# A decoder layer's cross-attention: ScalarE writes the key mask into PSUM in eight of twelve score slots

## The chip, the core and the metric

The kernel runs on one core of a Trainium2 chip. The time is the device time of one execution in microseconds (us). The core has five engines that run their own instruction streams and meet at semaphores: TensorE (PE: matmul; PEld: its weight loads), VectorE (DVE), ScalarE (ACT), GpSimd (POOL) and SyncE (SP, which here issues the DMAs). A matmul writes PSUM, which has 8 banks.

## What is computed

32 sequences ("rows" below) of 112 tokens and width 256 pass through a decoder layer: a delta-rule attention with an MLP, a cross-attention over 375 context positions with 16 heads of 16, and a mixture of 6 experts with top-2 routing beside a shared expert. The change is in the cross-attention:

```python
x = x + attn(layernorm(x))
# cross-attention, 16 heads of width 16
Q, K, V = split(h @ wq.T), split(ctx @ wk.T), split(ctx @ wv.T)
scores = Q @ K.T / sqrt(16)
scores = where(mask == 1, -1e9, scores)          # mask: (32, 112, 375)
x = x + (softmax(scores) @ V) @ w_out.T
x = x + shared(h3) + top2_of_6_experts(h3)
```

## The kernel before

The cross-attention stage takes the rows one after another, about 19 us each, from 501 us to 1094 us of the profiled span. The scores are built transposed, keys on partitions: 375 keys are three chunks of 125, 16 heads are four groups of four, so a row has 12 **slots** (`SLOTS`), each a score tile of 125 keys x (4 heads x 112 queries) = 448 columns in one PSUM bank. Even slots use bank 0, odd slots bank 1.

In each slot PE (`mask_scores`, L1127 on, matmul at L1137) first multiplies `negbig` (a diagonal of -2^40, bf16) by `flagk` (the mask of this key chunk as 0 or 1, repeated over 4 heads), which opens the bank's accumulation with the masked value. Two matmuls of 224 columns (`score`, L1142) then add the scores of two head pairs each. ScalarE (`exponentials`, L1644) turns the tile into exponentials in SBUF (`pr`, six buffers). After four slots PE multiplies them by the values (`weighted_values`, L1156; in slots 1, 5 and 9 of the stream, for the four slots that lie one to four before). The mask matmul of slot q has to wait until the exponentials of slot q-2, which read the same bank, are done.

Each engine's order is written out by hand in its `step`. Into the slots of row r PE weaves, in fixed places, work of its neighbours: 16 row-maximum matmuls (L1122) for row r+1, whose tiles VectorE reduces (L2174); the projections of keys (L873 in slots 1 and 2), queries (slot 5, L1091) and values (slot 8, L873) for row r+2; and the end of row r-1: the transpose of its values' sum (slot 3, L1170), the transpose of its normalised output (slot 6, L1177) and the output projection (slot 7, `project_out`, L1184). PE runs its stream strictly in this order, so a wait in front of one of these holds up all that stands behind it.

ScalarE's order in a row, one place after another:

- slot 0: hT copy (L1660), exp 0; slot 1: exp 1, the copy of the values' sum (L1649), high half of the keys 0 (L1619)
- slot 2: exp 2, high half of the keys 1; slot 3: exp 3, the gate's exp (L1664); slot 4: exp 4, h2T copy (L1623)
- slot 5: exp 5, high half of the queries (L1627); slot 6: exp 6, onT copy (`copy_on`, L1653), for which the output projection waits
- slot 7: exp 7; slot 8: exp 8, negated maxima (L1638), values (L1632)
- slot 9: values (L1634), high half of the context (L1542), exp 9; then exp 10 and exp 11

VectorE makes the low half of keys 1 (`klo`, L2160) out of ScalarE's high half; the transpose of h in slot 4 (L1083) waits for that.

The last row (row 31) has no row after it, so there are no row maxima in it, and ScalarE has six more instructions in its slots 3 to 8 (`high_expert`, L1676, a weight piece each, which GpSimd or VectorE then splits). Behind row 31 come the routing of the last rows, the plan of the expert blocks and the experts.

Of the kernel before, what the change touches and what calls it, by code (L numbers as in the profile page):

```python
# [33 lines left out]
ACT = mybir.ActivationFunctionType  # L34
# [7 lines left out]
B, T, D = 32, 112, 256  # L42
# [20 lines left out]
G = B // GB  # L63
GT = GB * T
# [3 lines left out]
KP = S2 // KC  # L68
# [4 lines left out]
LEVELS = (2, 4, 8, 16, 32, 64)  # L73
SLOTS = KC * HEADS // 4
PROBS = 6
BIG = float(2 ** 40)
# [4 lines left out]
RB = 3  # L81
ROUNDS = (B - 3) // RB
DENSE = (3, 7)
HPB = 4
FIRST_MAXIMA = 2
MAXIMA = ((0, 0, 0, 0), (1, 1, 1, 0), (1, 1, 0, 1), (0, 1, 0, 0), (1, 0, 0, 0), (1, 1, 1, 0), (1, 0, 0, 1), (0, 1, 0, 0))
LN_EPS, RMS_EPS = 1e-5, 1e-6

# [35 lines left out]
def decoder_layer(nc, io, out):  # L124
    with ExitStack() as ctx:
# [3 lines left out]
        def sem(name):  # L129
            return ctx.enter_context(nc.semaphore(name))  # L130
# [3 lines left out]
        bank = [psum[:, i, :] for i in range(8)]  # L134
# [89 lines left out]
        with ExitStack() as scope:  # L224
# [18 lines left out]
            flagk = w2("flagk", [KP, RB, KC, T], BF16)  # L243
# [16 lines left out]
        with ExitStack() as scope:  # L260
# [42 lines left out]
        s = {n: sem(n) for n in names + [f"stage{i}" for i in range(STAGES)]}  # L303
        s2 = {n: sem("c_" + n) for n in """cleared ctx_in c_hi c_lo mask_in ready bn flags stat rs h hT_ps hT_sb q_ps q_hi q_lo k_ps k_hi k_lo v01_ps v_ps v_sb qst0 qst1 qst2 kst0 kst1 kst2
            max_ps smax mt_ps negm negm_in sc_ps exp pv_done pv_sb ot_ps rden on onT_ps onT_sb wo_ps x_new""".split()}
# [72 lines left out]
        def heads_at(q, place):  # L378

            n = FIRST_MAXIMA + sum(sum(x) for x in MAXIMA[:q]) + sum(MAXIMA[q][:place])  # L380
            return range(n, n + MAXIMA[q][place])

# [12 lines left out]
        def ahead(t, par, rows):  # L395

            return t + (par + rows) // RB, (par + rows) % RB
# [459 lines left out]
        def _(pe):  # L857
# [250 lines left out]
            def row_max(t, par, heads):  # L1108

                n = t * RB + par  # L1110
                for hd in heads:
                    if hd == 0:
                        pe.wait_ge(s2[f"qst{par}"], filled("qst", t))
                        pe.wait_ge(s2[f"kst{par}"], filled("kst", t))
                        if not is_row(n, 0):
                            pe.wait_ge(s2["negm"], n)
                        if not isinstance(n, int) or n >= 4:
                            pe.wait_ge(s["h1"], G + n - 2)
                    freed = 2 if is_row(n, 0) else 3
                    if hd >= freed:  # L1120
                        pe.wait_ge(s2["smax"], HEADS * n + hd - freed + 1)
                    pe.matmul(bank[max_bank(n, par, hd)][0:T, 0:S2E], head(qst[par][0:ROWS], hd), pair(kst[par][0:ROWS], hd // 2), start=True, stop=True).then_inc(s2["max_ps"], 1)  # L1122
# [6 lines left out]
            def mask_scores(t, par, q):  # L1129

                b = t * RB + par
                if q == 0:
                    pe.wait_ge(s2["negm_in"], 16 * (b + 1))
                    pe.wait_ge(s2["flags"], b + 1)
                pe.wait_ge(s2["exp"], SLOTS * b + q + 2)
                flags = flagk[:, par, q // HPB, :].unsqueeze(1).broadcast_to([KP, HPB, T])
                pe.matmul(bank[q % 2][0:KP, 0:GT], negbig[:], flags, start=True, stop=False, skip_group_check=True)  # L1137
# [78 lines left out]
            def step(t, par, first=False, following=2):  # L1216
# [3 lines left out]
                if following >= 1:  # L1220
                    row_max(*nxt, range(FIRST_MAXIMA))
                if early >= 2:
                    transpose_row(*ahead(t, par, -2))
                for q in range(SLOTS):

                    maxima = following >= 1 and q < len(MAXIMA)
                    mask_scores(t, par, q)
                    for i in range(HPB // 2):
                        score(t, par, q, i)
# [241 lines left out]
        def _(act):  # L1471
# [65 lines left out]
            def high_context(t, par):  # L1537
                f = t * RB + par
                act.wait_ge(s2["ctx_in"], 16 * (f + 1))
                if not is_row(f, 0):  # L1540
                    act.wait_ge(s2["v_ps"], f)
                nc.scalar.copy(chi[:, :, 0:S2], ctxT[:]).then_inc(s2["c_hi"], 1)  # L1542
# [69 lines left out]
            def high_k(t, par, m):  # L1612
                f = t * RB + par
                act.wait_ge(s2["k_ps"], DC * f + m + 1)
                if m == 0 and not is_row(f, 0):
                    before = ahead(t, par, -1)
                    act.wait_ge(s2[f"kst{before[1]}"], filled("kst", before[0]))
                    act.wait_ge(s2[f"qst{before[1]}"], filled("qst", before[0]))
                nc.scalar.copy(khi[:, m], bank[DENSE[m]][:, 0:S2E]).then_inc(s2["k_hi"], 1)  # L1619

            def copy_h(t, par):
                act.wait_ge(s2["hT_ps"], t * RB + par + 1)
                nc.scalar.copy(h2T[:], bank[DENSE[1]][:, 0:2 * T]).then_inc(s2["hT_sb"], 1)  # L1623
# [5 lines left out]
            def copy_v(t, par, part):  # L1629
                act.wait_ge(s2[("v01_ps", "v_ps")[part]], t * RB + par + 1)  # L1630
                if part == 0:
                    nc.scalar.copy(vaug[par][:, 0:2, :, 0:HD], bank[DENSE[1]][0:KP, :].rearrange("k (c h d) -> k c h d", c=2, d=HD)).then_inc(s2["v_sb"], 1)  # L1632
                else:
                    nc.scalar.copy(vaug[par][:, 2, :, 0:HD], bank[DENSE[0]][0:KP, 0:D].rearrange("k (h d) -> k h d", d=HD)).then_inc(s2["v_sb"], 1)  # L1634
# [5 lines left out]
            def exponentials(t, par, q):  # L1640
                done = SLOTS * (t * RB + par) + q
                act.wait_ge(s2["sc_ps"], done + 1)
                act.wait_ge(s2["pv_done"], done + 1)
                nc.scalar.activation(pr[q % PROBS][:].rearrange("k i q -> k (i q)"), bank[q % 2][0:KP, 0:GT], ACT.Exp, scale=1.0 / HD ** 0.5).then_inc(s2["exp"], 1)  # L1644

            def copy_pv(t, par):
                p = t * RB + par
                act.wait_ge(s2["pv_done"], SLOTS * (p + 1) + PROBS)
                nc.scalar.copy(pv[:], bank[6][:, 0:GT]).then_inc(s2["pv_sb"], 1)  # L1649
# [5 lines left out]
            def keep_h(t, par):  # L1655
                r = t * RB + par
                act.wait_ge(s["ht_ps"], G + r + 1)
                if not isinstance(r, int) or r >= 3:
                    act.wait_ge(s3["sent"], 16 * (r - 1))
                nc.scalar.copy(hT3[par][:], bank[DENSE[0]][:, 0:2 * T]).then_inc(s3["hall"], 1)  # L1660
# [17 lines left out]
            def step(t, par, first=False, following=2, context=True):  # L1678
                early = t * RB + par if isinstance(t, int) else RB
                prev, nxt, far = ahead(t, par, -1), ahead(t, par, 1), ahead(t, par, 2)  # L1680
                for q in range(SLOTS):
                    if q == 0 and early >= 2:
                        keep_h(*ahead(t, par, -2))
                    if q == 9 and following >= 2:
                        copy_v(*far, 1)
                    if q == 9 and context:
                        high_context(*ahead(t, par, 3))
                    exponentials(t, par, q)
                    if q == 1 and not first:
                        copy_pv(*prev)  # L1690
                    if q in (1, 2) and following >= 2:
                        high_k(*far, q - 1)
                    if q == 4 and following >= 2:
                        copy_h(*far)
                    if q == 5 and following >= 2:
                        high_q(*far)
                    if q == 6 and not first:
                        copy_on(*prev)
                    if q == 8 and following >= 1:
                        negate_max(*nxt)  # L1700
                    if q == 8 and following >= 2:
                        copy_v(*far, 0)
                    if q == 3 and early >= 2:
                        exponential_gate(*ahead(t, par, -2))
                    if early == 1 and q in (5, 7, 9):
                        high_expert((q - 5) // 2)
                    if following == 0 and 3 <= q < 3 + NE:
                        high_expert(q)
# [136 lines left out]
        def _(dve):  # L1845
# [344 lines left out]
            def step(t, par, first=False, following=2, norm=True):  # L2190
# [4 lines left out]
                if following >= 1:  # L2195
                    maxima(*nxt, range(FIRST_MAXIMA))
                for q in range(SLOTS):
                    for place in range(4):
# [7 lines left out]
                        if place == 0 and q == 3 and following >= 2:  # L2206
                            low_k(*far, 1)
                        if following >= 1 and q < len(MAXIMA):
                            maxima(*nxt, heads_at(q, place))
# [279 lines left out]
```

## Time and profile before

| | before |
|---|---|
| time, median of 3 runs | 1362.65 us (1361.55 to 1363.04) |
| time of the profiled execution | 1365.04 us |
| its span, first to last instruction | 1363.0 us |
| PE busy / PE weight loads busy | 1260.6 us (92%) / 1146.1 us (84%) |
| DVE / ACT / POOL busy | 906.5 (67%) / 652.5 (48%) / 511.7 us (38%) |
| mean granted TensorE clock | 0.974 |

Busy time adds up the durations of an engine's instructions, and for PE overlapping matmuls are joined. An instruction's duration is its own latency, not what it costs the engine: in the timeline the next one often starts before it ends. A start of one to the start of the next is the cost. The chain of waits is the path of work that ended last, and gives each instruction on it only the time by which it held the path.

### The profile page before, as it was taken

The page shows a single profiled execution, that of the slowest core. Times are in us where ns is not written, and L with a number is a line of the kernel's source. Part 1 is how long each engine was busy: PE and PEld are TensorE (multiplying, and loading weights), DVE is VectorE, ACT ScalarE, POOL GpSimd, SP SyncE. Part 2 cuts the span into 40 slices and gives each one's busy share as a digit, 9 for nine tenths or more (in the row PEclk, how much of TensorE's full clock was granted, in tenths as well). Part 3 has the DMA queues.
Part 4 walks back from the last instruction along what each step waited for, and adds up shares of the span by engine and source line. Part 5 has one row for each costly group of instructions (what it writes and reads, how often), then busy time and mean ns, then how long its engine had stood idle before and what let it go on. Part 6 is the DMA issues. An engine that isn't in the chain of part 4 may idle for free.

```text
span 1363.0 us, 34519 instructions
## 1 busy us (share of the span) xinstructions
PE 1260.6 (92%) x11122; PEld 1146.1 (84%) x11122; DVE 906.5 (67%) x2932; ACT 652.5 (48%) x1524; POOL 511.7 (38%) x709
## 2 busy tenths in 40 slices
PE   4899999999989779999999999999999987999994
PEld 4789989889878678998999999999999876888883
DVE  3785674764854557777777777777777576655547
ACT  3443344334333325555555555555555653555540
POOL 2332241331431243244443444444344361333336
PEclk9999999999999889999999999999999998999997
DMA  8499600000000334555555555555555343333358
GB/s 200 107 236 240 149 0 0 0 0 0 0 12 11 87 103 120 147 143 142 129 140 132 144 142 133 131 135 144 142 140 145 76 136 86 99 106 101 102 137 247
DMA packets 131262, 151.39 MB, mean 111 GB/s; under 512 B 41107, under 2 KB 111108, under 8 KB 131156
## 3 DMA queue, kind: packets, MB, share of 16 engines
q1 hardware_dynamic: 124436, 134.55, 40.4%
q0 software_dynamic: 6160, 15.69, 3.4%
q8 instruction: 42, 0.69, 0.2%
q14 instruction: 48, 0.39, 0.1%
q10 hardware_dynamic: 576, 0.07, 0.0%
HBM read 79.27 MB, written 45.82 MB: 92 GB/s over the span
## 4 chain that ended last, share of the span: by engine, by line
PE 51%; DVE 4%; DMA 2%; POOL 2%; issue 2%; SPq 1%; ACT 1%; DVEq 0%; POOLq 0%; ACTq 0%
PE psum L873 9%; PE psum L1122 7%; PE psum L1156 6%; PE psum L1142 6%; PE psum L1137 5%; PE psum L1291 5%; PE psum L1311 3%; PE psum L1184 2%; PE psum L1091 2%; PE psum L1203 1%; PE psum L1170 1%; DMA e_hi<-routed_y 1%; DVE x_res L2310 1%; PE psum L1282 1%; PE psum L1299 1%
## 5 line engine op out<-in xcount | busy, mean ns | idle before, releaser
L2174 DVE CUSTOM_DVE_ANT_0 junk<-psum,biasq 112x375 f32<-112x375 f32 x512 | 269.5, 542 | 109.8 <-issue 90.8
L1644 ACT ACTIVATE pr<-psum 125x448 f32<-125x448 f32 x384 | 205.5, 545 | 79.8 <-PE psum L1142 72.8
L1142 PE MATMUL psum<-qst,kst 97*125 97x224 f32 x768 | 224.8, 353 | 0.0
L1122 PE MATMUL psum<-kst,qst 96*112 96x376 f32 x512 | 170.5, 356 | 4.0 <-DVE smax L2174 2.7
L1142 PEld LDWEIGHTS psum<-qst,kst 97*125 97x125 f32 x768 | 146.1, 190 | 6.7
L1137 PE MATMUL psum<-flagk,negbig 125*125 125x448 bf16 x384 | 138.9, 362 | 3.1 <-ACT pr L1644 2.8
L715 POOL TENSOR_TENSOR rs<-rs,neg_half 112x1 f32<-112x1 f32 x32 | 18.2, 569 | 276.7 <-DVE rs L2087 276.7
L839 POOL DMA_INDIRECT routed_y<-yb,yrow x61 | 58.5, 960 | 123.8 <-ACT yb L1821 117.8
L1122 PEld LDWEIGHTS psum<-kst,qst 96*112 96x112 f32 x512 | 89.2, 179 | 13.5 <-issue 6.9
L1156 PE MATMUL psum<-pr,vaug 125*32 125x112 f32 x3072 | 94.4, 263 | 0.0
L1156 PEld LDWEIGHTS psum<-pr,vaug 125*32 125x32 f32 x3072 | 70.9, 110 | 15.8 <-issue 6.1
L757 POOL DMA_INDIRECT routed_h<-h,slot x64 | 66.2, 1034 | 32.5 <-POOL h L746 14.8
L1562 ACT COPY xq<-psum 112x224 f32<-112x224 f32 x80 | 27.0, 347 | 86.0 <-PE psum L981 84.0
L2405 DVE TENSOR_TENSOR hidb<-sgb,psum 128x256 f32<-128x256 f32 x61 | 25.7, 421 | 62.9 <-ACT sgb L1806 62.9
L666 POOL TENSOR_TENSOR cT<-negT,masks_sb 112x448 f32<-112x448 f32 x48 | 61.3, 1304 | 7.9 <-DVE negT L1947 7.9
L1137 PEld LDWEIGHTS psum<-flagk,negbig 125*125 125x125 bf16 x384 | 52.5, 137 | 11.3 <-issue 6.1
L981 PE MATMUL psum<-tri,cT 112*112 112x112 f32 x320 | 40.7, 269 | 19.1 <-DVE triT L1952 10.9
L1619 ACT CAST khi<-psum 128x376 fp32r<-128x376 f32 x64 | 30.1, 472 | 56.3 <-PE psum L873 56.3
L981 PEld LDWEIGHTS psum<-tri,cT 112*112 112x112 f32 x320 | 36.7, 180 | 22.8 <-POOL cT L666 13.3
L1509 ACT CAST hidhi<-hid 128x448 fp32r<-128x448 f32 x32 | 18.1, 566 | 75.4 <-DVE hid L1922 75.4
L710 POOL TENSOR_SCALAR biasq<-maskq 112x375 f32<-112x375 int32 x32 | 50.3, 1571 | 9.0 <-DMA maskk<-in_maskT 5.8
L994 PE MATMUL psum<-xq,triT 112*112 112x112 f32 x320 | 49.2, 279 | 3.7 <-ACT xq L1562 3.2
(319 smaller groups left out, 3520.7 us busy)
## 6 DMA issues: line engine op xcount, KB each, us to landing
kst<-khi SPq DMA_DIRECT2D x64, 376.0 KB, 4.6
routed_h<-in_route_pad SPq DMA_DIRECT2D x6, 3640.0 KB
kst<-klo SPq DMA_DIRECT2D x32, 376.0 KB, 6.1
ctxT<-in_ctxT SPq DMA_DIRECT2D x32, 375.0 KB, 3.5
hblk<-routed_h SPq DMA_DIRECT2D x61, 130.0 KB, 2.1
qst<-qhi SPq DMA_DIRECT2D x128, 56.0 KB, 2.4
stage<-in_e SPq DMA_DIRECT2D x21, 256.0 KB, 3.3
maskq<-in_mask SPq DMA_DIRECT2D x32, 164.1 KB
```

The source lines that it names most:

```text
L666: nc.gpsimd.tensor_tensor(cT[:, n], negT[:], over_rows(M_BT + 1 + n), op=ALU.mult).then_inc(s["cmask"], 1)
L757: pool.indirect_dma_start(hbuf[:, :], to, h3[par][:], None).then_inc(s3["scat"], 16)
L839: pool.indirect_dma_start(ybuf[:, :], to, yb[:, u], None).then_inc(s4[f"out{u}"], 16)
L873: mm = pe.matmul(to, st, mv, start=n == 0, stop=n == len(products) - 1)
L981: mm = pe.matmul(bank[6 + u][0:T, cols(j % 2)], cT[:, n, j], tri[:, j], start=True, stop=True)
L1122: pe.matmul(bank[max_bank(n, par, hd)][0:T, 0:S2E], head(qst[par][0:ROWS], hd), pair(kst[par][0:ROWS], hd // 2), start=True, stop=True).th ...
L1137: pe.matmul(bank[q % 2][0:KP, 0:GT], negbig[:], flags, start=True, stop=False, skip_group_check=True)
L1142: mm = pe.matmul(bank[q % 2][0:KP, cols(i, 2 * T)], pair(kst[par], n)[:, cols(q // HPB, KP)], both(qst[par], n), start=False, stop=True, s ...
L1156: mm = pe.matmul(bank[6][row:row + 2 * HD, cols(hd // HPB)], vaug[par][:, c3, hd], pr[q % PROBS][:, i], start=q == 0, stop=c3 == KC - 1, s ...
L1291: mm = pe.matmul(bank[4 + u][0:BLK, :], hp, e13[wp][:, bass.ds(e, 1), c].rearrange("p a w n -> p (a w n)"), start=n == 0, stop=n == len(pa ...
L1644: nc.scalar.activation(pr[q % PROBS][:].rearrange("k i q -> k (i q)"), bank[q % 2][0:KP, 0:GT], ACT.Exp, scale=1.0 / HD ** 0.5).then_inc(s ...
L2174: nc.vector.tensor_tensor_reduce(out=junk[:, hd % 2, :], in0=bank[max_bank(n, par, hd)][0:T, 0:S2], in1=biasq[:, par, :], scale=1.0, scala ...
```

## The change

A new constant `WRITTEN` names slots 3 to 10. In these PE's mask matmul is gone. Instead ScalarE, right behind the exponentials of slot q-2, which was the last reader of the bank, writes `flags * -2^40` into the bank (`write_mask`, 125 partitions x 448 fp32 elements, from the bf16 flags with the repetition over 4 heads in the access pattern), and PE's first score matmul of the slot waits for that on the semaphore `cmask`. Both score matmuls already ran with `start=False`, that is they add onto the bank. Slots 0, 1, 2 and 11 keep the mask matmul. `write_mask` begins with a wait on ScalarE's own semaphore `exp`: for the completion of the exponentials that ScalarE has just issued.

```diff
+WRITTEN = range(3, 11)
@@ PE, mask_scores
                 if q == 0:
                     pe.wait_ge(s2["negm_in"], 16 * (b + 1))
                     pe.wait_ge(s2["flags"], b + 1)
+                if q in WRITTEN:
+                    pe.wait_ge(s["cmask"], G * len(LEVELS) + len(WRITTEN) * b + q - WRITTEN[0] + 1)
+                    return
                 pe.wait_ge(s2["exp"], SLOTS * b + q + 2)
                 flags = flagk[:, par, q // HPB, :].unsqueeze(1).broadcast_to([KP, HPB, T])
                 pe.matmul(bank[q % 2][0:KP, 0:GT], negbig[:], flags, start=True, stop=False, skip_group_check=True)
@@ ScalarE
+            def write_mask(t, par, q):
+
+                b = t * RB + par
+                if q == WRITTEN[0]:
+                    act.wait_ge(s2["flags"], b + 1)
+                act.wait_ge(s2["exp"], SLOTS * b + q + 2)
+                flags = flagk[:, par, q // HPB, :].unsqueeze(1).broadcast_to([KP, HPB, T])
+                nc.scalar.activation(bank[q % 2][0:KP, 0:GT].rearrange("k (i q) -> k i q", i=HPB), flags, ACT.Copy, scale=-BIG).then_inc(s["cmask"], 1)
@@ ScalarE, step
                     exponentials(t, par, q)
+                    if q + 2 in WRITTEN:
+                        write_mask(t, par, q + 2)
                     if q == 1 and not first:
                         copy_pv(*prev)
```

## Rows read from the trace of the kernel before

**Rows 1.** The page, parts 1 and 2: busy time; granted clock in 40 slices.
```profile
PE 1260.6 (92%) x11122; PEld 1146.1 (84%) x11122; DVE 906.5 (67%) x2932; ACT 652.5 (48%) x1524; POOL 511.7 (38%) x709
PEclk9999999999999889999999999999999998999997
```
**Rows 2.** Busy time by window, one stretch: us, PE, PEld, DVE, ACT, POOL; clock; DMA.
```profile
800.00:850.00 50.00, 49.83 (x553) 45.53 (x551) 37.25 (x149) 29.74 (x66) 25.21 (x45) 1.00 0.52 133
```
**Rows 3.** PE's waits, 500 to 1100 us, the longest: us in total, times, longest.
```profile
PE psum L1137 <- ACT pr L1644: 2.8, 2, 2.3
```
**Rows 4.** Chain of waits in one row of the stage: start us, us held.
```profile
763.60 0.19 PE psum L1137
...
765.46 0.19 PE psum L1137
765.65 0.21 PE psum L1142 x2
...
782.26 0.19 PE psum L1137
```
**Rows 5.** Timeline of PE, the same row: slots 3, 5, 6, 9, 11 (L1137), two waiters.
```profile
772.05 0.35 PE L1137 MATMUL psum<-flagk,negbig 125*125 125x448 bf16 x1
...
773.65 0.35 PE L1083 MATMUL psum<-ident_sb,h 112*128 112x112 f32 x2
773.84 0.35 PE L1137 MATMUL psum<-flagk,negbig 125*125 125x448 bf16 x1
...
776.74 0.35 PE L1137 MATMUL psum<-flagk,negbig 125*125 125x448 bf16 x1
...
778.35 1.12 PE L1184 MATMUL psum<-xwo_sb,onT 128*112 128x256 f32 x4
...
782.10 0.35 PE L1137 MATMUL psum<-flagk,negbig 125*125 125x448 bf16 x1
...
783.96 0.35 PE L1137 MATMUL psum<-flagk,negbig 125*125 125x448 bf16 x1
```
**Rows 6.** Timeline of ACT, the same row: keys 1, exp 3, exp 6, onT, exp 9.
```profile
772.08 0.47 ACT L1619 CAST khi<-psum 128x376 fp32r<-128x376 f32 x1 [0.65 <-PE psum L873]
772.66 0.54 ACT L1644 ACTIVATE pr<-psum 125x448 f32<-125x448 f32 x1
...
777.51 0.54 ACT L1644 ACTIVATE pr<-psum 125x448 f32<-125x448 f32 x1 [0.23 <-PE psum L1142]
777.95 0.34 ACT L1653 COPY onT<-psum 128x224 f32<-128x224 f32 x1
...
783.29 0.55 ACT L1644 ACTIVATE pr<-psum 125x448 f32<-125x448 f32 x1
```
**Rows 7.** Timeline of DVE, the same row: klo, and two dependent instructions.
```profile
772.87 0.54 DVE L2160 TENSOR_TENSOR klo<-psum,khi 128x376 fp32r<-128x376 f32 x1
...
774.35 0.25 DVE L2181 RECIPROCAL rden<-psum 112x16 f32<-112x16 f32 x1
774.64 0.42 DVE L2183 TENSOR_TENSOR on<-psum,rden 112x256 f32<-112x256 f32 x1
```
**Rows 8.** The page, part 5: groups of instructions, xcount, busy, mean ns.
```profile
L1644 ACT ACTIVATE pr<-psum 125x448 f32<-125x448 f32 x384 | 205.5, 545 | 79.8 <-PE psum L1142 72.8
...
L1137 PE MATMUL psum<-flagk,negbig 125*125 125x448 bf16 x384 | 138.9, 362 | 3.1 <-ACT pr L1644 2.8
...
L1509 ACT CAST hidhi<-hid 128x448 fp32r<-128x448 f32 x32 | 18.1, 566 | 75.4 <-DVE hid L1922 75.4
```
**Rows 9.** Groups by line, 480 to 1110 us: a copy of 448 elements out of PSUM.
```profile
L1649 ACT COPY pv<-psum 128x448 f32<-128x448 f32 x32 | 17.1, 533 | 18.3 <-PE psum L1156 18.3
```
**Rows 10.** Timeline of ACT in the last row: first weight piece, and onT.
```profile
1084.75 0.65 ACT L1676 CAST e_hi<-stage 128x512 fp32r<-128x512 f32 x1
...
1087.59 0.41 ACT L1653 COPY onT<-psum 128x224 f32<-128x224 f32 x1
```
**Rows 11.** Timeline of POOL behind it: what the next stage's chain waits for.
```profile
1090.79 0.57 POOL L715 TENSOR_TENSOR rs<-rs,neg_half 112x1 f32<-112x1 f32 x1 [1.57 <-DVE rs L2087]
```

## The prediction, made before the changed kernel was run

> **What bounds the kernel now.** I read four views in this order. First the page: PE is busy for 92% of the span and its granted clock stands near 1.0 through the cross-attention [rows 1]. Then the windows: in 50 us of the middle of that stage PE is busy for 49.83, DVE for 37.25, ACT for 29.74 [rows 2]. Then PE's waits: over 600 us the longest entry is 2.8 us [rows 3]. So nothing holds PE up there, it is the bound, and what is taken from its stream is time gained, as long as nobody else becomes late. Last the chain of waits: for a whole row it stays on PE, and tells what each instruction costs the stream. The mask matmul holds it for 0.19 us, two score matmuls for 0.21 together [rows 4]; the 362 ns of the groups [rows 8] are latency, and a saving reckoned from them would be twice too large. A row is 782.26 - 763.60 = 18.66 us [rows 4].
>
> **What is taken away.** Eight of twelve mask matmuls a row: 8 x 0.19 = 1.52 us a row, 32 x 1.52 = 48.6 us in all, if PE stays the only bound. (The count of 384 is 12 in each of 32 rows [rows 8].)
>
> **What is added.** Eight ACT instructions a row. Nothing in the trace writes PSUM from bf16 flags in SBUF. The nearest rows of 448 elements are a copy out of PSUM, 533 ns [rows 9], exp out of PSUM, 545 ns, and a cast from SBUF to SBUF, 566 ns [rows 8]. I take 0.55, and 0.45 to 0.60 as bounds, the lower one because no row shows ACT writing into PSUM, and it can be cheaper. In ACT's stream the next instruction starts about 0.10 before the last one ends (exp 6 at 777.51 lasts to 778.05, onT starts at 777.95) [rows 6]. But `write_mask` waits for the end of the exp just issued, so this overlap is lost. A dependent instruction follows 0.04 after the end of the one before it on DVE (774.35 + 0.25, then 774.64) [rows 7]; for ACT I take 0.05, bounds 0.03 to 0.12. So each write moves all that stands behind it on ACT by 0.10 (overlap lost) + 0.05 (self-wait) + 0.55 (write) - 0.10 (its own overlap with the next) = 0.60 us. ACT goes from 0.59 of the time [rows 2] by 8 x 0.60 = 4.8 us of 18.66 to about 0.85. That is below 1, yet it is now in line with PE four times a row, so I go through these places. From ACT's end to PE's start I allow 0.06, from 777.95 + 0.34 to 778.35 [rows 5, 6].
>
> **Slots 3 to 5** (masks 3, 4 and 5 gone, -0.57). ACT's keys 1 cast at 772.08 stays where it is, since no mask removed lies before it; exp 3 then starts at 772.48 instead of 772.66 and ends at 773.02; the write for slot 5 ends at 773.02 + 0.05 + 0.55 = 773.62, PE sees it at 773.68. PE itself would be there at 773.84 - 0.38 = 773.46. A second wait ahead of it: the transpose in slot 4, at 773.65 - 0.38 = 773.27, needs `klo`, which ends at 773.41 [rows 7]. So slot 5 starts 0.22 late: net -0.57 + 0.22 = -0.35.
>
> **Slots 6 and 7, up to the output projection** (masks 6 and 7 gone, one of them at the start of the stretch). From slot 6's start, 776.74, to the projection, 778.35, is 1.61 us [rows 5]. It starts just as ACT's onT copy ends (778.29), so it has no slack. After: exp 6 starts 777.51 - 776.74 - 0.19 = 0.58 in, ends at 1.13, the write ends at 1.73, onT runs from 1.63 to 1.97 and PE goes on at 2.03. PE's own work would be there at 1.61 - 0.38 = 1.23. It waits 0.80 us, and the stretch is 0.42 longer than before. The write sits between exp 6 and the copy for which PE waits, and is needed itself only a projection later. This is the largest term.
>
> **Slot 8.** Nothing on ACT is waited for: -0.19.
>
> **Slots 9 to 11** (masks 9 and 10 gone). Slot 11 keeps its mask matmul, which waits for exp 9. ACT gets to exp 9 only behind the values and context casts, which start from PE's last value projection, ahead of slot 9. So it ends at 783.29 + 0.55 = 783.84, PE can start slot 11 at 783.90, and did at 783.96 [rows 5, 6]. Of 0.38 taken away only 0.06 is gained.
>
> **The sum of a row**: -0.35 + 0.42 - 0.19 - 0.06 = -0.18 us instead of -1.52. Rows 1 to 29: 29 x -0.18 = -5.2. Row 0 has no output projection of a row before, but its slots 3 to 8 are short, so each write falls late there as well: 0. Row 30 gains in slots 9 to 11, where no context cast stands, and loses more in slots 3 to 5, where PE has less to do: -0.1. **Row 31**: ACT has its weight pieces between the exponentials and is without a gap up to onT at 1087.59 [rows 10]; six writes stand ahead of that, 6 x 0.60 = +3.6. The projection behind onT leads over VectorE to GpSimd's rs, which stood waiting for it [rows 11], and on to the routing of the last rows and the plan, where no engine is full; I take it to reach the end (bounds +2 to +4). Sum: -5.2 - 0.1 + 3.6 = -1.7 us. DMAs: none is added or moved in its queue; ACT's query cast, for which SP waits, follows exp 5 only after a pause in which PE projects the queries, and the write for slot 7 fits into that.
>
> The Trainium skill ("ScalarE: Activation LUTs", What ACT_TABLE_LOAD costs) gives 186 ns + 0.833 ns an element for an ACTIVATE with immediate scale, 559 ns for 448, as an estimate from that page; exp's 545 ns [rows 8] agrees within 3%, and the sum would move by under 0.5 us a stage.
>
> **Against the times.** The profiled execution took 1365.04, its span 1363.0, the median of three is 1362.65. I put -1.7 on the median: 1360.9 us.
>
> **The rivals.**
> A, the forecast: the gain is paid back in waits for ACT. 1357 to 1365.
> B, a quicker write. The two large waits hang on write and self-wait together, twice a row: 0.10 less gives -0.20 a row. With 0.45 + 0.05 that is 29 x -0.38 = -11.0, and +3.0 at row 31: -8, 1354.7 us. For it: ACT's read port into PSUM is what the rows show, its write port is not. The Trainium skill ("ScalarE: Activation LUTs", Step-by-step: what each stage is for) says that ScalarE's way into PSUM is faster than into SBUF; by that rule B is what happens. No row of this trace shows a ScalarE write to PSUM.
> C, PE stays the bound: the waits of slots 5, 7 and 11 are hidden, because the starts that the trace gives for PE hide slack. -48.6 + 3.6, 1318 us. Against it: the projection starts 0.06 behind onT, the mask of slot 11 0.12 behind exp 9 [rows 5, 6], each without slack.
> D, slower: the self-wait drains ACT for more than I allow. Each 0.10 adds 0.20 a row. From 0.69 for write and self-wait together (I have 0.60) a row gains nothing; at 0.80, +0.22 a row, 29 x 0.22 = +6.4, and +4.8 at row 31 give +11, 1374 us; at 0.70, +0.6 + 4.2, 1367.5 us. For it: no instruction of ACT in this stage waits for ACT, so the price rests on a row of DVE.
> E, the change doesn't do what it says: were the writes overwritten by the scores, the same instructions would run, and the time be A's.
>
> **Chances.** A 0.50, B 0.18, C 0.06, D 0.26 (E within A). A measurement of this kernel can tell about 0.2%, 2.7 us, from no change. A's own range straddles that bound: two fifths of it, 0.18, count as faster, 0.28 as same, and 0.04 as slower. B and C are faster but for 0.02. D is slower but for 0.04. Faster 0.18 + 0.16 + 0.06 = 0.40; same 0.28 + 0.02 + 0.04 = 0.34; slower 0.04 + 0.22 = 0.26. The range leaves out C, the low end of B and the high end of D: 1352 to 1370.
>
> **What would show it.** In the waits of PE: the output projection (L1184) waits for ACT's onT about 0.8 us in some 30 rows, 24 us in all, the slot 11 mask for ACT's exp some 9 us, the transpose in slot 4 and the scores of slot 5 some 7 us; PE's busy time in the stage drops from full to about 0.93, ACT's rises to 0.8 or more. The row period is 18.5. The write's mean is 550 ns, and the exp before it ends 0.05 ahead of it. If the projection's wait isn't there, A is wrong and C right; if the write's mean is under 500 ns, B; if the gap in front of it is over 0.15, D. Row 31's onT should come 3.6 us later, counted from the start of that row; if the end of the kernel doesn't move with it, the term of row 31 is wrong.

## The result and the profile after

The changed kernel is slower: 1368.27 us (median of 14 runs, 1365.47 to 1372.91) against 1363.55 us of the kernel before (14 runs). The ratio is 1.0041, 95% interval 1.003 to 1.0051. Two later comparisons gave 1.0025 (1.0014 to 1.0037) and 1.0025 (1.0012 to 1.0037). The loss is 3 to 5 us, where 1.7 us of gain was forecast.

The page of the changed kernel, busy time:

```profile
PE 1235.4 (91%) x10866; PEld 1106.0 (81%) x10866; DVE 906.3 (66%) x2932; ACT 783.9 (57%) x1780; POOL 507.1 (37%) x709
...
L1657 ACT ACTIVATE psum<-flagk 125x448 f32<-125x448 bf16 x256 | 140.2, 548 | 8.6
```

PE has lost 25 us of busy time and its 256 matmuls, against [rows 1]; ACT has gained 131 us. One write takes 548 ns, where 550 was taken. The windows show where PE's saving went. In the middle of the stage, to be set beside [rows 2]:

```profile
800.00:850.00 50.00, 47.73 (x532) 42.05 (x530) 37.89 (x157) 39.96 (x86) 21.85 (x38) 1.00 0.58 142
```

PE fell from 49.83 to 47.73 of 50 us, and ACT rose from 29.74 to 39.96. PE now stands still for a part of each row. Its waits from 480 to 1130 us name the place; in the kernel before, the longest entry was 2.8 us [rows 3]:

```profile
PE psum L1188 <- ACT onT L1666: 23.4, 31, 1.1
PE psum L1146 <- ACT psum L1657: 2.3, 5, 0.6
PE psum L1141 <- ACT pr L1648: 2.3, 1, 2.3
```

31 waits of the output projection for the onT copy. (L1188 is L1184 of the kernel before, L1146 the scores, L1141 the mask matmul, L1657 the write, L1666 the onT copy.) The two timelines of one row, PE and ACT, slots 6 to 11; the last number is the idle time before the instruction:

```profile
772.89 0.35 PE L1146 MATMUL psum<-qst,kst 97*125 97x224 f32 x1
...
775.02 1.12 PE L1188 MATMUL psum<-xwo_sb,onT 128*112 128x256 f32 x4 [0.73 <-ACT onT L1666]
...
779.78 0.48 PE L1146 MATMUL psum<-qst,kst 97*125 97x224 f32 x2
780.36 0.40 PE L1141 MATMUL psum<-flagk,negbig 125*125 125x448 bf16 x1
```
```profile
773.57 0.55 ACT L1648 ACTIVATE pr<-psum 125x448 f32<-125x448 f32 x1
774.14 0.55 ACT L1657 ACTIVATE psum<-flagk 125x448 f32<-125x448 bf16 x1
774.63 0.34 ACT L1666 COPY onT<-psum 128x224 f32<-128x224 f32 x1
...
779.04 0.82 ACT L1546 CAST chi<-ctxT 128x750 fp32r<-128x750 f32 x1
779.76 1.08 ACT L1648 ACTIVATE pr<-psum 125x448 f32<-125x448 f32 x2
```

Exp 6 ends at 774.12, and the write begins 0.02 us later. The copy that PE waits for begins behind the write. From slot 6 to the projection are 2.13 us, where it was 1.61 [rows 5]. In the chain of waits of the same row ScalarE now appears, where before there was PE alone, at this place and at slot 11:

```profile
773.57 0.55 ACT pr L1648
774.12 0.02 issue
774.14 0.03 ACT psum L1657
...
774.63 0.35 ACT onT L1666
774.97 0.04 issue
775.02 1.12 PE psum L1188 x4
...
779.76 0.56 ACT pr L1648
780.31 0.04 issue
780.36 0.40 PE psum L1141
```

The waits view counts the first of these but not the second: ahead of slot 11 PE's last instruction is modelled as still running, so it shows no idle time. The chain shows it.

To cut a row up I took the starts of landmark instructions in PE's timeline, in 23 rows of each profile, and their distances (medians; the third is a mean, since at the end of each third row, where PE's loop turns, some 0.4 us are added). The last two columns are experiments that are told below. The rows to look at first are slot 7's, where the change loses, and slot 10's.

| stretch of PE's stream | masks in it | before | after | five: copy first, last row without writes | four: masks removed, no writes |
|---|---|---|---|---|---|
| projection to values of r+2 | 8 | 1.36 | 1.17 | 1.17 | 1.17 |
| to the values matmuls of slot 9 | 9 | 2.90 | 2.70 | 2.71 | 2.71 |
| to the transpose ahead of slot 0 | 10 | 2.25 | 2.41 | 2.41 | 2.42 |
| router to the transpose in slot 3 | 3 | 4.21 | 4.04 | 4.04 | 4.03 |
| to the transpose in slot 4 | 4 | 1.01 | 1.02 | 1.01 | 1.01 |
| to the values matmuls of slot 5 | 5 | 1.03 | 0.93 | 0.93 | 0.91 |
| query projection to slot 6's transpose | 6 | 1.46 | 1.28 | 1.28 | 1.28 |
| to the projection | 7 | 1.03 | 1.65 | 1.03 | 1.03 |
| 27 rows, projection to projection | | 507.08 | 505.50 | 489.07 | 488.76 |

The rows themselves are 1.6 us shorter in all. The loss is behind them: from row 30's slot 7 (1071.86 us) to row 31's slot 7 are 15.39 us instead of 11.93, and from there to the last projection 14.44 instead of 13.54, together 4.36 us. The growth of the second is the clock. In these windows of the changed kernel the granted clock is 0.63 and 0.69, between the levels of 1.2 and 2.4 GHz; in the kernel before it was 1.00 in both:

```profile
1080.00:1090.00 10.00, 7.96 (x58) 5.90 (x56) 2.79 (x11) 9.36 (x21) 4.21 (x4) 0.63 0.31 96
1090.00:1100.00 10.00, 9.44 (x95) 7.69 (x94) 7.85 (x15) 4.49 (x10) 8.52 (x14) 0.69 0.14 33
```

PE had waited for ScalarE's writes before the clock fell: 0.45, 0.37 and 0.56 us in front of three slots, and the projection in row 31's slot 7 starts 1.07 us late and takes 2.04 us instead of 1.12, about the 0.90 by which the last stretch grew. Over all profiles the two go together: in the seven with seven or eight writes in the last row this projection runs at the low clock, takes 1.89 to 2.05 us, and the last stretch is 14.31 to 14.48. In the ten with one write or none it takes 1.12 us and the stretch is 13.53 to 13.67. That PE's pauses bring the clock down is the likely reading; nothing was run that has the pauses alone.

### The profile page after: what moved, and what is told of

Same layout as the page of the kernel before. It is cut to its first block, busy times and chain, and to the rows that moved or that the text cites. A ratio compares the mean times of both kernels' runs of the same rounds, so it can differ in the third digit from the quotient of the medians.

```text
span 1364.4 us, 34463 instructions
## 1 busy us (share of the span) xinstructions
PE 1235.4 (91%) x10866; PEld 1106.0 (81%) x10866; DVE 906.3 (66%) x2932; ACT 783.9 (57%) x1780; POOL 507.1 (37%) x709
## 4 chain that ended last, share of the span: by engine, by line
PE 49%; ACT 4%; issue 4%; DVE 3%; DMA 2%; POOL 1%; SPq 1%; ACTq 0%; DVEq 0%; POOLq 0%
PE psum L874 9%; PE psum L1123 6%; PE psum L1160 6%; PE psum L1295 6%; PE psum L1146 5%; PE psum L1315 3%; ACT pr L1648 3%; PE psum L1188 3%; PE psum L1141 2%; PE psum L1092 2%; PE psum L1338 1%; PE psum L1207 1%; PE psum L1174 1%; DVE x_res L2325 1%; PE psum L1286 1%
## 5 line engine op out<-in xcount | busy, mean ns | idle before, releaser
L1146 PE MATMUL psum<-qst,kst 97*125 97x224 f32 x768 | 206.8, 324 | 2.3 <-ACT psum L1657 2.3
L1146 PEld LDWEIGHTS psum<-qst,kst 97*125 97x125 f32 x768 | 141.1, 192 | 13.7 <-issue 5.8
L1657 ACT ACTIVATE psum<-flagk 125x448 f32<-125x448 bf16 x256 | 140.2, 548 | 8.6
L758 POOL DMA_INDIRECT routed_h<-h,slot x64 | 66.2, 1034 | 32.2 <-POOL h L747 14.8
L1188 PE MATMUL psum<-xwo_sb,onT 128*112 128x256 f32 x128 | 36.6, 410 | 23.4 <-ACT onT L1666 23.4
L982 PEld LDWEIGHTS psum<-tri,cT 112*112 112x112 f32 x320 | 37.1, 182 | 23.4 <-POOL cT L667 13.3
L1821 ACT ACTIVATE sgb<-psum 128x256 f32<-128x256 f32 x61 | 23.4, 383 | 56.8 <-PE psum L1295 56.8
L1141 PE MATMUL psum<-flagk,negbig 125*125 125x448 bf16 x128 | 47.9, 374 | 5.3 <-ACT pr L1648 2.3
```

What stands on the lines that cost most here:

```text
L758: pool.indirect_dma_start(hbuf[:, :], to, h3[par][:], None).then_inc(s3["scat"], 16)
L982: mm = pe.matmul(bank[6 + u][0:T, cols(j % 2)], cT[:, n, j], tri[:, j], start=True, stop=True)
L1146: mm = pe.matmul(bank[q % 2][0:KP, cols(i, 2 * T)], pair(kst[par], n)[:, cols(q // HPB, KP)], both(qst[par], n), start=False, stop=True, s ...
L1188: mm = pe.matmul(bank[DENSE[0]][0:T, 0:D], onT[:, c], xwo[:, c], start=c == 0, stop=c == DC - 1)
L1657: nc.scalar.activation(bank[q % 2][0:KP, 0:GT].rearrange("k (i q) -> k i q", i=HPB), flags, ACT.Copy, scale=-BIG).then_inc(s["cmask"], 1)
```

## The experiments

All edits are against the changed kernel unless said otherwise. Ratios are to the kernel before, run on the same chip in turn.

**One: the onT copy ahead of the write.** The theory was ScalarE's order; the rival, that the writes cost something everywhere.

```diff
                     exponentials(t, par, q)
+                    if q == 6 and not first:
+                        copy_on(*prev)
                     if q + 2 in WRITTEN:
                         write_mask(t, par, q + 2)
...
-                    if q == 6 and not first:
-                        copy_on(*prev)
```

> In slot 6 ScalarE does the onT copy ahead of the write for slot 8; all else as in the changed kernel. Theory (ScalarE's order): the stretch from slot 6 to the output projection falls from 2.13 us to about 1.42 (exp 6 starts 0.58 in, plus 0.44, 0.34 and 0.06), so a row gets shorter by 0.6 to 0.7, 29 rows by 17 to 20 us, and the last row has one write less ahead of its onT, -0.6: 1368 - 19 = 1349 us, ratio to the kernel before 0.99. PE's wait for onT (23.4 us) goes nearly to nothing. Rival (what the writes cost is spread over all of them, as contention in PSUM or a slower stream of PE): moving one write by one place changes nothing, 1366 to 1370 us.

Ratio 0.9921 (0.9901 to 0.994). On other chips I repeated it:

> The onT copy ahead of the write in slot 6, last row with its writes. Theory: 28 rows x 0.62 = 17 us less than the changed kernel, ratio to the kernel before 0.990 to 0.992; with both edits it was 0.9888, so the last row is worth 0.2 to 0.3%. Rival (last row absorbed): the same 0.9888.

Ratio 0.9911 (0.9896 to 0.9925), 1350.64 us beside 1365.41 us of the changed kernel: 14.8 us less, where 17 were forecast. In the steady rows the whole gain is in one stretch: the projection's from 1.65 to 1.03 us, 0.62 a row. The rival is out: one write moved by one place in ScalarE's stream turns a loss of 0.25 to 0.4% into a gain of 0.8 to 0.9%.

**Two: one write alone.**

```diff
-WRITTEN = range(3, 11)
+WRITTEN = (8,)
```

The count on `cmask` that PE waits for is adapted, here and in experiment three.

> ScalarE writes the mask in slot 8 alone; eleven mask matmuls stay in each row. Theory (the write for slot 8 sits between exp 6 and the onT copy that PE waits for, and is paid there): exp 6 starts 0.77 after slot 6, write ends 1.90 after it, onT 2.14, PE goes on at 2.20 instead of 1.61: +0.59 - 0.19 = +0.40 a row, 29 rows +11.6, the last row +0.6: 1376 us, ratio 1.009. One eighth of the change costs more than the whole. Rival (each write costs the same share of the 4.7 us): +0.6 us, 1364 us, ratio 1.0005.

Ratio 1.0105 (1.0084 to 1.0126): +14.5 us, where 12 were forecast, and more than the whole change costs. In its profile the projection's stretch is 1.65 us again and slot 8's 1.17, so a row loses 0.62 and gains 0.19. The waits of this kernel, 540 to 1040 us:

```profile
PE psum L1188 <- ACT onT L1666: 13.5, 25, 0.6
PE psum L874 <- DVE logit L2112: 9.8, 23, 0.7
```

The first line is the expected one. The second has nothing to do with the change; it is told under the hardware.

**Three: all but that write.** `WRITTEN = (3, 4, 5, 6, 7, 9, 10)`.

> ScalarE writes the mask in slots 3 to 7, 9 and 10, not in 8. Theory: no write stands ahead of onT in slot 6. Slot 6 to the projection falls to 1.42, slot 8 keeps its mask matmul (+0.19): a row is 0.5 shorter than before, 29 rows -14.5, the last row +3 and what its clock costs +1, the first row +1: about 1354 us, ratio 0.993. PE's wait for onT is gone but in the last rows. Rival (spread cost): seven eighths of +4.7, 1367.6 us, ratio 1.0035.

Ratio 0.9968 (0.9953 to 0.9982). The sign and the mechanism are right, the wait for onT is gone from its profile, but the gain is 4.4 us and not 9.5. On the same chip it is 6.6 us slower than experiment one (1375.90 against 1369.28). Slot 8's mask matmul, which it keeps, has 0.19 us a row in its stretch (1.36 against 1.17), which by 29 rows is 5.5 us; the rest of the shortfall was not followed up.

**Four: the masks removed and nothing put in their place.** This kernel leaves the mask out in slots 3 to 10, so it computes less. It is the most that the removal can bring as long as all else keeps its order.

```diff
                 if q in WRITTEN:
-                    pe.wait_ge(s["cmask"], ...)
+                    pe.wait_ge(s2["exp"], SLOTS * b + q + 2)
                     return
...
-                mm = pe.matmul(..., start=False, stop=True, ...)
+                mm = pe.matmul(..., start=i == 0 and q in WRITTEN, stop=True, ...)
...
-                    if q + 2 in WRITTEN:
-                        write_mask(t, par, q + 2)
```

> The mask is left out in slots 3 to 10: no mask matmul, and no write; the first score matmul opens the bank, after PE's old wait for the exponentials. Theory (PE is the only bound without the writes): 8 x 0.19 a row, 32 rows, 45 to 49 us: 1316 us, ratio 0.966. Rival (ScalarE's exponentials, with their latency, hold PE in slots 9 to 11 and at the onT copy even without the writes): the row gains 1.52 less 0.3 for slots 9 to 11 and 0.2 at the projection, 32 us: 1332 us, ratio 0.976.

Ratio 0.9863 (0.9848 to 0.9878), 1344.59 us. Both numbers were wrong, and this run corrects the picture most: without any write a row gets 0.68 us shorter and not 1.52. The table shows where the rest stays. The masks of slots 9 and 10 together give 0.02 (-0.19 in the first of their stretches, +0.17 in the next, where slot 11 waits for exp 9). Slot 4's gives nothing: PE waits there for `klo`, which is told further below. Nor does slot 7's, ahead of the projection. Slot 5's gives 0.12. PE was busy for 49.83 of 50 us before [rows 2], and even so more than half of what was taken out of its stream did not arrive.

**Five: the copy first, and no writes in the last row.** On one chip with the changed kernel and the kernel before:

```diff
-                if q in WRITTEN:
+                if q in WRITTEN and not is_row(b, B - 1):
...
+                    if q == 6 and not first:
+                        copy_on(*prev)
-                    if q + 2 in WRITTEN:
+                    if q + 2 in WRITTEN and following >= 1:
...
-                    if q == 6 and not first:
-                        copy_on(*prev)
```

> The onT copy ahead of the write in slot 6, and no writes in the last row. Theory (ScalarE's order): the gain of the copy's place, 18 us against the changed kernel, and the last row's 3 to 4: 1363.5 x (1 - 0.0125) = 1347 us, ratio 0.987 to 0.990. Rival (the last row is absorbed by what stands behind it): as with the copy's place alone, 0.992.

> The kernel before, unchanged, for a profile on the same chip as the runs beside it. Theory: the row period and the stretches between PE's landmarks are those of the first profile of before (18.78 us a row). Rival (the chip of the earlier runs was different in the stage itself): the stretch from the router's matmul to the transpose in slot 3, 4.21 us in the first profile, is about 0.7 us longer here too.

> The changed kernel, unchanged. Theory (a small loss, most of it in the last row and in its clock): ratio 1.002 to 1.006. Rival (the loss depends on the chip): outside of that, and a row period that differs from the kernel before by more than 0.1 us.

1347.97 us, ratio 0.9888 (0.9873 to 0.9903). The kernel before had its row of 18.78 us again, the changed one 1.0025. In this kernel's rows nothing is left of the writes' cost: all its stretches are those of experiment four within 0.02 us. ScalarE does 248 writes in this kernel (31 rows by 8). From 560 to 1050 us PE waits for none of them; in the whole profile it waits 0.8 us for them. ScalarE's stream in slot 6, and the projection:

```profile
771.15 0.54 ACT L1648 ACTIVATE pr<-psum 125x448 f32<-125x448 f32 x1
771.59 0.34 ACT L1666 COPY onT<-psum 128x224 f32<-128x224 f32 x1
771.82 0.57 ACT L1657 ACTIVATE psum<-flagk 125x448 f32<-125x448 bf16 x1
```
```profile
771.99 1.12 PE L1188 MATMUL psum<-xwo_sb,onT 128*112 128x256 f32 x4
```

The copy's end at 771.93 still sets the projection's start. That is why the mask of slot 7 gives nothing even here.

**Six: the last row.** First alone, then beside the changed kernel:

> As the changed kernel, but the last row keeps its twelve mask matmuls and has no writes. Theory (the last row is bound by ScalarE, and its waits let TensorE's granted clock fall): the granted clock between 1080 and 1100 us goes back from 0.63 and 0.69 to 1.0, the stretch between the last two output projections but one from 15.4 to 12 us, the last from 14.4 to 13.5, in all 4 us less than the changed kernel: 1364 us, ratio to the kernel before 1.000. Rival (the last row's delay is absorbed by the routing behind it): within 1 us of the changed kernel, ratio 1.004.

Ratio 1.0047 (1.003 to 1.0064). That is against the theory, and it can't be held against the changed kernel, which had not run on that chip.

> The changed kernel without writes in the last row, now beside the changed kernel on the same chip. Theory (the last row's delay reaches the end): 3.5 to 4.5 us less than the changed kernel, ratio to the kernel before 0.999 to 1.001 (rows -1.5, first rows +1). Rival (absorbed by the routing behind it, or given back by the clock): within 1 us of the changed kernel.

> The changed kernel, unchanged, on one chip with the two variants beside it. Ratio to the kernel before 1.002 to 1.006.

> The kernel before, unchanged, for a profile on the chip of the three runs beside it. Were this the chip of the first four runs (before at 1378 us), the theory that the chip itself holds PE in slots 1 and 2 wants the stretch from the router's matmul to the slot 3 transpose near 4.9 us instead of 4.21, and a row of 19.5 us, in this kernel too; otherwise 18.78 us.

Ratios 1.0011 (0.9997 to 1.0024) without writes in the last row and 1.0025 (1.0012 to 1.0037) with them, and medians of 1365.31 and 1365.41 us. In the profiles the effect on the last row is plain. The two stretches are 11.67 and 13.54 us again, and the granted clock at 1080 us is back:

```profile
1080.00:1090.00 10.00, 8.94 (x131) 7.62 (x131) 5.14 (x20) 8.79 (x20) 7.55 (x10) 1.00 0.37 116
```

In the times it does not show beyond doubt. So the same edit once more, on top of the copy's new place, both beside each other on one chip:

> onT copy ahead of the write in slot 6, no writes in the last row. Ratio to the kernel before 0.9888 as before. Against the run beside it with last-row writes: theory (the last row's delay reaches the end) 3 to 4.5 us less, 0.25 to 0.3%; rival (absorbed) within 1 us.

> onT copy ahead of the write in slot 6, the last row with its writes. Theory 0.991 to 0.992 of the kernel before, rival (the last row's delay is absorbed) 0.9888.

0.9889 (0.9873 to 0.9905) without last-row writes, 1347.3 us; 0.9908 (0.989 to 0.9926) with them, 1350.82 us. Three comparisons (0.14, 0.23 and 0.19%, the second across two chips: 0.9911 against 0.9888) go the same way, each with intervals that overlap. The last row costs some 2 to 3 us at the kernel's end, by these; whether the 4.4 us of the two stretches arrive in full stays open. The profiles show nothing that would give them back: from the last projection to the end of the span are 259.4 to 262.7 us in the five profiles of these chips with writes in the last row, and 257.8 to 261.5 in the eight without. But that scatter is nearly as large as the delay.

**Seven: exp 9 ahead of the context cast,** against experiment five. It tests the forecast's step for slots 9 to 11.

```diff
-                    if q == 9 and context:
-                        high_context(*ahead(t, par, 3))
                     exponentials(t, par, q)
...
+                    if q == 9 and context:
+                        high_context(*ahead(t, par, 3))
```

> As e5b, and in slot 9 ScalarE does exp 9 ahead of the context's high half (822 ns). Theory (slot 11's mask waits for exp 9): exp 9 starts about 0.5 us earlier, the stretch from the values matmuls of slot 9 to the transpose ahead of the next row falls from 2.41 to about 2.1 us, 29 rows x 0.3 = 9 us, ratio 0.982. Rival 1 (something else holds slot 11, such as the values matmuls or the maxima on VectorE): the stretch stays 2.41, ratio 0.9888. Rival 2 (the context's halves come too late for the key projection of the next row): the gain is given back in slot 1, PE waits there for VectorE's clo, ratio 0.988 or above.

1336.15 us, ratio 0.9816 (0.9791 to 0.9841). The stretch fell from 2.42 to 1.99 us, and PE shows no new wait in slot 1. Two gains are in that. In most rows it was 2.28 to 2.31 us and is 1.98 now, the 0.3 that were forecast. In each third row, where PE's loop turns, it was 2.67 and is 1.98 as well: the loop's 0.4 us are gone too, though the loop is the same. That the loop is paid only behind PE's wait in slot 11 is likely, and not tested by itself. ScalarE's stream in slot 9, and PE's slots 10 and 11:

```profile
715.36 0.37 ACT L1638 COPY vaug<-psum 125x256 f32<-125x256 f32 x1
715.63 0.55 ACT L1648 ACTIVATE pr<-psum 125x448 f32<-125x448 f32 x1
716.07 0.82 ACT L1546 CAST chi<-ctxT 128x750 fp32r<-128x750 f32 x1
```
```profile
716.37 0.48 PE L1146 MATMUL psum<-qst,kst 97*125 97x224 f32 x2
716.69 0.35 PE L1141 MATMUL psum<-flagk,negbig 125*125 125x448 bf16 x1
```

Slot 11's mask matmul now starts 0.32 us behind slot 10's scores, where it was 0.58 (779.78 to 780.36). This kernel beats both kernels, the kernel before by 26 us (1362.38 beside it), and even experiment four, which has no mask at all in these slots.

## Why the prediction was wrong

**The sign hung on a small difference of large terms.** Per row, by the forecast's own steps, with what the table gives:

| step | forecast | measured |
|---|---|---|
| slots 3 to 5 | -0.35 | -0.17 + 0.01 - 0.10 = -0.26 |
| slots 6 and 7 | +0.42 | -0.18 + 0.62 = +0.44 |
| slot 8 | -0.19 | -0.19 |
| slots 9 to 11 | -0.06 | -0.20 + 0.16 = -0.04 |
| sum | -0.18 | -0.05 |

The mechanism held for the largest term, in engine, instruction and size: 0.44 for 0.42, and 23.4 us of waits in 31 rows for "24 us in some 30". It held in slots 8 to 11 too. The write took 548 ns for 550, the wait on ScalarE's own semaphore 0.02 to 0.03 us for 0.05. PE's busy share in the window came to 0.95 for 0.93, ACT's to 0.80 as forecast. **The term that was mis-sized most is slots 3 to 5**, -0.26 for -0.35, and a part of its mechanism was wrong.

The forecast let PE wait 0.22 us for the write for slot 5. A wait of that length is there, but it is the one for `klo` in slot 4, which the forecast had named as its second: masks 3 and 4 give 0.16 instead of 0.38, without any writes as well (0.18). Before, PE's transpose of h started 0.24 us behind `klo` [rows 5, 7]. In the changed kernel, and in experiment four, the second fence, it starts 0.05 us behind it:

```profile
769.39 0.55 DVE L2175 TENSOR_TENSOR klo<-psum,khi 128x376 fp32r<-128x376 f32 x1
769.99 0.41 PE L1084 MATMUL psum<-ident_sb,h 112*128 112x112 f32 x2
```
```profile
767.12 0.54 DVE L2173 TENSOR_TENSOR klo<-psum,khi 128x376 fp32r<-128x376 f32 x1
767.71 0.41 PE L1084 MATMUL psum<-ident_sb,h 112*128 112x112 f32 x2
```

The write for slot 5 ends at 770.11, just in time for slot 5's scores at 770.17. These stand 0.18 us behind the transpose, with writes and without.

The other part is the price of the mask itself. I had taken each removed mask at 0.19 us, from the chain [rows 4]. Slot 5's gives 0.10, and 0.12 in experiment four, so the write has at most 0.02 us of part in it. There the first score matmul costs PE 0.19 to 0.20 us where it cost about 0.10 behind the mask matmul. That its weight load had been hidden by the mask's 448 columns is the likely reading; it was not tested alone.

Over 27 rows the sum came to -1.6 us, which for 29 rows is -1.7, and -5.2 was forecast. That is 3.5 us of the miss, most of it from slots 3 to 5.

**The last row** was forecast at +3.6 and measured at 3.46 to the projection, its size right. What was missing is what stands behind it: the clock. PE's pauses there were followed by a granted clock of 0.63, and the last stretch took another 0.90 us. The forecast has no term for it; before, the clock stood at 1.00 through this part of the page.

**The first rows** were put at 0. From the first score to the projection in row 2's slot 7 are 51.72 us before and 52.49 after, +0.8. Both kernels were seen longer there as well: 55.46 in one of three profiles of the kernel before, 58.22 and 58.45 in two of three of the changed kernel. The clock goes with it. Over the 60 us from 495 us on, the granted clock is 0.91 in both first profiles, 0.89 in the one with 55.46, and 0.80 and 0.83 in the two with 58. The changed kernel, first profile and the one beside experiment six:

```profile
495.00:555.00 60.00, 52.76 (x530) 45.75 (x528) 42.84 (x143) 43.76 (x91) 22.34 (x28) 0.91 0.51 128
```
```profile
495.00:555.00 60.00, 51.74 (x469) 44.54 (x468) 39.91 (x134) 41.14 (x85) 18.76 (x22) 0.83 0.47 121
```

The changed kernel's executions spread over 7.4 us, those of the kernel before over 5.7. That these first rows make the spread is likely and not shown.

**The sum**: rows -1.6, last row +3.5 and +0.9, first rows +0.8 or more: +3.6 us, where 1.7 less was forecast and 3 to 5 more was measured. The spans of the two first profiles differ by 1.4 us only, since the part ahead of the stage, which the change doesn't touch, took 3.4 us less in the second (501.49 against 498.06 us to the first score), and the part behind the last projection 1.3 us more, which is within its scatter. The time lies within the range of 1352 to 1370; the direction, at 0.26 for slower, was the wrong one.

**The rivals.** B, a quicker write, fell: it needed 450 ns, and 548 were measured. The Trainium skill ("ScalarE: Activation LUTs", Step-by-step: what each stage is for) has ScalarE's way to PSUM as the faster one. The rows here give that at most a few per cent: the write is 18 ns shorter than the cast of as many elements from SBUF to SBUF (566 ns [rows 8]), and 6 ns longer than the exponentials out of PSUM in the same profile (542). The Trainium skill's formula ("ScalarE: Activation LUTs", What ACT_TABLE_LOAD costs) gives 559 ns as an estimate, within 2% of the measured. (By the forecast's own steps those 9 ns would have moved its sum by 0.6 us, not by under 0.5.) C, PE as the only bound, fell by more than its own measure: not even without any writes are the 48.6 us to be had, only 19. D, a dear self-wait, fell as a mechanism, at 0.03 us where it needed 0.14; the time went its way for other reasons.

## What to carry to other kernels

Work taken off the engine that is busy all the time is gained only as far as the next wait in its stream. Walk the stream and ask at each removed piece who is just in time behind it; here that left 0.68 of 1.52 us a row. Work moved to an idle engine costs nothing where no one waits for what stands behind it there, and its full length where someone does: the same 256 writes lost 3 to 5 us, or gained 12, by the place of one of them. In experiment seven more went than the wait that it was aimed at: the loop's 0.4 us in each third row too. When stretches of the kernel with different neighbours (first row, last row) are summed with the steady ones, look there for the clock as well.

## What the runs showed of the hardware

**A chip on which the stage itself is slower.** The four kernels of experiments one (first run), two, three and six (first run) ran on a chip where the kernel before took 1378.34 us. In all four profiles the router-to-transpose stretch is 4.7 to 4.9 us instead of 4.04 to 4.21, and PE waits there for VectorE's logits, 8.1 to 10.5 us in 500 us of the stage, a wait that no profile of the other chips has. In slot 1 VectorE starts on PE's row maximum 1.9 us behind the matmul's start, where it is 0.58 on other chips, and ScalarE's copy of the values' sum starts 2.0 us behind the end of the values matmuls instead of 0.07. Why they start late was not found. Nor do all ratios carry over: for experiment one they agree (0.9921 there, 0.9911 and 0.9908 elsewhere), but for the changed kernel without writes in the last row they do not (1.0047 there, 1.0011 elsewhere, and the intervals do not meet). So the sizes of experiments two and three, which ran on that chip alone, may differ by as much elsewhere, some 5 us. That leaves the sign of experiment two, and the projection's stretch in both profiles, but the gain of experiment three is shown for that chip only.

**The cost of a wait on one's own semaphore** on ScalarE: 0.02 to 0.03 us beyond the end of the instruction waited for (0.09 in eight of the 256 writes), and the loss of the 0.10 us by which two instructions overlap otherwise.
